# A decoder layer on one core: in the routed expert tiles, gate and up weights become the stationary operand, and the down product gets a second bank

## What is computed

```python
def _L0_ffn_ref(hidden_states, gate_w, sh_gate, sh_up, sh_down, rt_gate, rt_up, rt_down):
    x = hidden_states.reshape(-1, h)
    logits = x @ gate_w
    top_val = jnp.max(logits, axis=-1, keepdims=True)
    top_id = jnp.argmax(logits, axis=-1)
    score = jax.nn.sigmoid(top_val)
    xs = x * score
    g = jnp.einsum('th,ehi->eti', xs, rt_gate)      # H=128, I=256, E=8
    u = jnp.einsum('th,ehi->eti', xs, rt_up)
    act = jax.nn.silu(g) * u
    y = jnp.einsum('eti,eih->eth', act, rt_down)
    onehot = jax.nn.one_hot(top_id, E, dtype=x.dtype)
    routed = jnp.einsum('eth,te->th', y, onehot)
    shared = _swiglu(x, sh_gate, sh_up, sh_down)
    return (shared + routed).reshape(b, s, h)
```

## Time and profile before

| | |
|---|---|
| median of three runs | 648.67 us |
| the profiled execution, and the span of its trace | 643.3 us, 641.6 us |
| TensorE (PE) busy, share of the span | 593.4 us, 92% |
| VectorE (DVE) | 428.0 us, 67% |
| ScalarE (ACT) | 424.9 us, 66% |
| GpSimd (POOL) | 310.7 us, 48% |
| tail loop, first record transpose to last output scatter | 549.57 to 633.07 us |

### The profile page before, as it was taken

How to read it: one execution, slowest core, us unless ns; L and a number is a source line. 1 busy time by engine, 2 the same in 40 slices (tenths; PEclk the granted TensorE clock), 3 DMA queues, 4 the chain that set the end, 5 groups by cost and what they waited for, 6 DMA issues and landing times.

```text
span 641.6 us, 14968 instructions
## 1 busy us (share of the span) xinstructions
PE 593.4 (92%) x5231; PEld 514.1 (80%) x5231; DVE 428.0 (67%) x1185; ACT 424.9 (66%) x1512; POOL 310.7 (48%) x331
## 2 busy tenths in 40 slices
PE   3868999999999999999999999999999987999993
PEld 2767799889988998899989988998889876766661
DVE  3858665878685868586858685868564566376562
ACT  3538788777776787678677867786768764444551
POOL 3524644365336633663366336633652354147553
PEclk9969999999999999999999999999999998899997
DMA  7300000000010001000100000000000007325420
GB/s 161 98 18 13 17 2 2 13 18 2 2 30 18 17 3 30 18 18 2 30 18 17 1 15 17 17 2 2 17 18 1 2 27 227 115 72 157 144 74 8
DMA packets 24953, 23.49 MB, mean 37 GB/s; under 512 B 7007, under 2 KB 22497, under 8 KB 24880
## 3 DMA queue, kind: packets, MB, share of 16 engines
q1 hardware_dynamic: 20368, 14.91, 8.6%
q0 software_dynamic: 2784, 6.32, 2.7%
q10 hardware_dynamic: 1728, 1.32, 0.9%
HBM read 15.03 MB, written 7.95 MB: 36 GB/s over the span
## 4 chain that ended last, share of the span: by engine, by line
PE 70%; DVE 15%; ACT 7%; issue 3%; DMA 1%; POOL 1%; SPq 0%; DVEq 0%; POOLq 0%
PE bank L1128 9%; PE bank L1275 9%; PE bank L1243 8%; PE bank L1130 7%; PE bank L1129 7%; PE bank L1253 7%; PE bank L1264 5%; PE bank L1355 4%; ACT prob L1031 4%; PE bank L1224 2%; PE bank L1380 2%; PE bank L1135 2%; DVE stats L648 2%; DVE mneg L816 2%; ACT oT L1041 2%
## 5 line engine op out<-in xcount | busy, mean ns | idle before, releaser
L1031 ACT ACTIVATE prob<-bank,mneg 128x128 f32<-128x128 f32 x512 | 182.0, 376 | 80.1 <-DVE mneg L816 79.9
L560 POOL TENSOR_TENSOR prob<-prob,rden 128x512 f32<-128x512 f32 x128 | 130.7, 1041 | 107.1 <-DVE rden L823 106.8
L1031 ACT ACTIVATION_READ_ACCUMULATOR prob<-bank,mneg 128x1 f32 x512 | 109.8, 214 | 0.0
L1037 ACT COPY probT<-bank 128x512 f32<-128x512 f32 x128 | 76.8, 600 | 36.7 <-PE bank L1253 36.6
L816 DVE TENSOR_REDUCE mneg<-bank 128x4 f32<-128x512 f32 x128 | 80.3, 669 | 18.5 <-PE bank L1243 18.4
L1253 PE MATMUL bank<-ident,prob 128*128 128x128 f32 x512 | 78.4, 276 | 5.5 <-POOL prob L560 4.7
L499 POOL TENSOR_TENSOR rstd<-var_eps,neg_half 128x4 f32<-128x4 f32 x24 | 24.7, 1029 | 114.6 <-DVE var_eps L653 114.6
L1243 PE MATMUL bank<-kT,qT 64*128 64x128 f32 x1024 | 74.4, 285 | 2.9 <-issue 1.7
L1243 PEld LDWEIGHTS bank<-kT,qT 64*128 64x128 f32 x1024 | 62.2, 187 | 14.0 <-issue 11.4
L1253 PEld LDWEIGHTS bank<-ident,prob 128*128 128x128 f32 x512 | 60.6, 142 | 10.6 <-issue 6.2
L1264 PE MATMUL bank<-probT,V 128*64 128x128 f32 x1024 | 64.2, 279 | 0.0
(11 more groups left out here) (194 smaller groups left out, 1332.9 us busy)
## 6 DMA issues: line engine op xcount, KB each, us to landing
prob<-routed SPq DMA_DIRECT2D x39, 128.5 KB, 2.1
xin<-in_x_dram SPq DMA_DIRECT2D x8, 256.0 KB, 2.8
ctx_nat<-in_ctx_dram SPq DMA_DIRECT2D x8, 192.0 KB, 2.5
routed<-blank ACTq DMA_DIRECT2D x8, 128.5 KB
qT<-in_L_ffn_rt_gate_dram SPq DMA_DIRECT2D x1, 1024.0 KB, 5.9
qT<-in_L_ffn_rt_up_dram SPq DMA_DIRECT2D x1, 1024.0 KB, 11.1
out_dram<-probT,prob POOLq DMA_INDIRECT x39, 2.2
prob<-in_L_xattn_Wq_dram SPq DMA_DIRECT2D x1, 512.0 KB, 6.1
```

The costliest lines, as they stand in the source:

```text
L560: nc.gpsimd.tensor_tensor(view, view, spread(rden[:, m % 2, c * NC:(c + 1) * NC], 2, S), ALU.mult)\
L1031: last = nc.scalar.activation(prob[:, m % 2, p * S:(p + 1) * S], score_bank(m, c)[:, i * S:(i + 1) * S], ACT.Exp, bias=mneg[:, m % 2, p:p ...
L1037: nc.scalar.copy(probT[:, m % 2, c * 512:(c + 1) * 512], made(r1, ("T", m, c))[:])\
```

## The change

ScalarE copies each tile's gate and up weights, 128x512, from where the register points to one of three fixed places (`w4`: the two halves of `xin`, and `hw`, which nothing uses any more by then). With the address fixed, the weights can be the stationary operand, in four pieces of 128 columns, and the turned record moves. The product then comes out with the hidden units on the partitions, which is how the down product wants the activation: the two transposes L1371 and the copy L1110 are gone. The three gate and up banks go round (`gu_bank`), the down product alternates between two banks, and so D of a tile waits for `y_done` of the tile two before it. ScalarE copies one tile ahead: `copy_weights(0)` stands ahead of its loop, and `copy_weights(j + 1)` between R and H of step `j`; each reads `exp_tab` into a register first. TensorE still reads it too, for the down weights.

```diff
@@ -215,8 +215,10 @@
         rec = prob[:].rearrange("p a n -> p (a n)")[:, 0:RING * ROW].rearrange("p (a b) -> p a b", a=RING)
         recT = oT[:, 0, 0:2 * P].rearrange("p (a b) -> p a b", a=2)
         tanh4 = oT[:, 0, 2 * P:2 * P + 2 * I].rearrange("p (a b) -> p a b", a=2)
-        act4 = V[:, 0, 0:2 * I].rearrange("p (a b) -> p a b", a=2)
-        act4T = V[:, 0, 2 * I:4 * I].rearrange("p (a b) -> p a b", a=2)
+        act4 = V[:, 0, 0:3 * I].rearrange("p (a b) -> p a b", a=3)
+
+        w4 = [xin[:, 0].rearrange("p b n -> p (b n)"), xin[:, 1].rearrange("p b n -> p (b n)"),
+              hw[:].rearrange("p b n -> p (b n)")]
         yo = probT[:, 0, 0:RING * D].rearrange("p (a b) -> p a b", a=RING)
 
         EVEN = XH * S // ROW
@@ -409,8 +410,8 @@
         TABLE_1, TAILS, TABLE_2 = 15, 16, 27
 
 
-        gu_bank = [bank[2], r1.bank(("PV", B - 1, 0))]
-        at_bank = [r1.bank(("PV", B - 1, 1)), r1.bank(("out", B - 1))]
+        gu_bank = [bank[2], r1.bank(("PV", B - 1, 0)), r1.bank(("PV", B - 1, 1))]
+        down_bank = [bank[1], r1.bank(("out", B - 1))]
 
         block = ctx.enter_context(nc.Block())
 
@@ -955,14 +956,14 @@
 
             def activate(j):
                 dve.wait_ge(gu_tanh, j + 1)
-                ps = gu_bank[j % 2]
-                if j >= 2:
-
-                    dve.wait_ge(at_ready, j - 1)
-                nc.vector.scalar_tensor_tensor(out=act4[:, j % 2], in0=tanh4[:, j % 2], scalar=1.0, in1=ps[:, 0:I],
+                ps = gu_bank[j % 3]
+                if j >= 3:
+
+                    dve.wait_ge(dn_ready, j - 2)
+                nc.vector.scalar_tensor_tensor(out=act4[:, j % 3], in0=tanh4[:, j % 2], scalar=1.0, in1=ps[:, 0:I],
                                                op0=ALU.add, op1=ALU.mult).then_inc(act_half, 1)
                 dve.wait_ge(act_half, j + 1)
-                nc.vector.scalar_tensor_tensor(out=act4[:, j % 2], in0=act4[:, j % 2], scalar=0.5,
+                nc.vector.scalar_tensor_tensor(out=act4[:, j % 3], in0=act4[:, j % 3], scalar=0.5,
                                                in1=ps[:, I:2 * I], op0=ALU.mult, op1=ALU.mult)\
                     .then_inc(act_done, 1)
 
@@ -970,7 +971,7 @@
                 dve.wait_ge(dn_ready, j + 1)
                 if j >= RING:
                     dve.wait_ge(out_in[j % RING], 16 * (j // RING))
-                nc.vector.tensor_tensor(yo[:, j % RING, :], bank[1][:, 0:D], rec[:, j % RING, D:2 * D],
+                nc.vector.tensor_tensor(yo[:, j % RING, :], down_bank[j % 2][:, 0:D], rec[:, j % RING, D:2 * D],
                                         ALU.add).then_inc(y_done, 1)
 
             for j in range(TILES + 3):
@@ -1093,21 +1094,33 @@
                     for g, step in steps_at(ACT_F, F_AT, n, b):
                         ffn(g, step)
 
+            def copy_weights(j):
+                if j >= 3:
+
+                    act.wait_ge(gu_ready, j - 2)
+                if j == ROUND1:
+                    act.wait_ge(table, TABLE_2)
+                half, i = (0, j) if j < ROUND1 else (1, j - ROUND1)
+                e = act.value_load(exp_tab[0:1, half, i:i + 1], min_val=0, max_val=E - 1)
+                nc.scalar.copy(w4[j % 3], rt_gu[:, bass.ds(e * (2 * I), 2 * I)]).then_inc(w4_in, 1)
+
+            act.wait_ge(table, TABLE_1)
+
+            act.wait_ge(x1_in, NG)
+            act.wait_ge(wr_in, 16 * 3)
+            copy_weights(0)
             for j in range(TILES + 3):
                 if j < TILES:
                     act.wait_ge(ft_ready, j + 1)
                     nc.scalar.copy(recT[:, j % 2], bank[0][:, 0:P]).then_inc(ft_copied, 1)
+                if j + 1 < TILES:
+                    copy_weights(j + 1)
                 if 0 <= j - 1 < TILES:
                     act.wait_ge(gu_ready, j)
                     if j >= 3:
                         act.wait_ge(act_done, j - 2)
-                    nc.scalar.activation(tanh4[:, (j - 1) % 2], gu_bank[(j - 1) % 2][:, 0:I], ACT.Tanh,
+                    nc.scalar.activation(tanh4[:, (j - 1) % 2], gu_bank[(j - 1) % 3][:, 0:I], ACT.Tanh,
                                          scale=0.5).then_inc(gu_tanh, 1)
-                if 0 <= j - 2 < TILES:
-                    act.wait_ge(at_ready, j - 1)
-                    if j >= 4:
-                        act.wait_ge(dn_ready, j - 3)
-                    nc.scalar.copy(act4T[:, j % 2], at_bank[j % 2][:, 0:I]).then_inc(at_copied, 1)
                 if j < 2:
                     empty_PV(B - 1, j)
                 for step in ACT_TAIL.get(j, ()):
@@ -1345,15 +1358,22 @@
                         pe.wait_ge(ft_copied, j)
                     pe.transpose(bank[0][:, 0:P], rec[:, j % RING, 0:D], ident[:]).then_inc(ft_ready, 1)
                 if 0 <= j - 1 < TILES:
-                    e = held[j - 1]
                     if j == 1:
 
                         pe.wait_ge(exp_done, NC * B)
                     if j == 2:
                         vacate(("PV", B - 1, 0))
+                    if j == 3:
+                        vacate(("PV", B - 1, 1))
                     pe.wait_ge(ft_copied, j)
-                    pe.matmul(gu_bank[(j - 1) % 2][:], recT[:, (j - 1) % 2], rt_gu[:, bass.ds(e * (2 * I), 2 * I)],
-                              start=True, stop=True).then_inc(gu_ready, 1)
+                    pe.wait_ge(w4_in, j)
+                    if j > 3:
+
+                        pe.wait_ge(act_done, j - 3)
+                    for c in range(2 * I // P):
+                        last = pe.matmul(gu_bank[(j - 1) % 3][:, c * P:(c + 1) * P], w4[(j - 1) % 3][:, c * P:(c + 1) * P],
+                                         recT[:, (j - 1) % 2], start=True, stop=True)
+                    last.then_inc(gu_ready, 1)
                 if j < TILES:
 
                     if j == ROUND1:
@@ -1363,21 +1383,16 @@
                     prob_v(B - 1, j)
                 if j == 2:
                     out_product(B - 1)
-                if 0 <= j - 2 < TILES:
-                    if j - 2 < 2:
-                        vacate((("PV", B - 1, 1), ("out", B - 1))[j - 2])
-                    pe.wait_ge(act_done, j - 1)
-                    for h in range(I // P):
-                        last = pe.transpose(at_bank[j % 2][:, h * P:(h + 1) * P],
-                                            act4[:, j % 2, h * P:(h + 1) * P], ident[:])
-                    last.then_inc(at_ready, 1)
                 if 0 <= j - 3 < TILES:
                     e = held.pop(j - 3)
-                    pe.wait_ge(at_copied, j - 2)
-                    if j > 3:
-                        pe.wait_ge(y_done, j - 3)
+                    pe.wait_ge(act_done, j - 2)
+                    if j == 4:
+                        vacate(("out", B - 1))
+                    if j > 4:
+
+                        pe.wait_ge(y_done, j - 4)
                     for h in range(I // P):
-                        last = pe.matmul(bank[1][:, 0:D], act4T[:, (j - 3) % 2, h * P:(h + 1) * P],
+                        last = pe.matmul(down_bank[(j - 3) % 2][:, 0:D], act4[:, j % 3, h * P:(h + 1) * P],
                                          rt_dn[:, bass.ds(e * I + h * P, P)], start=(h == 0),
                                          stop=(h == I // P - 1))
                     last.then_inc(dn_ready, 1)
```

More of the change, by code:

```diff
@@ L284, in decoder_layer @@
         act_done = sem("activation_done")
-        at_ready = sem("activation_turned")
-        at_copied = sem("activation_turned_copied")
+        w4_in = sem("tile_weights_copied")
         dn_ready = sem("down_ready")
```

## The result

The change made the kernel slower where the result was taken: 654.26 us (median of 6 runs, 652.47 to 656.96) against 648.49 us for the kernel before (6 runs, 648.15 to 649.01), ratio 1.0093, 95% interval 1.0066 to 1.012. Forecast were 645.4 us and a range up to 650.6. The runs of the changed kernel spread over 4.5 us, those of before over 0.9 us.

A forecast was written before the change was run, and what follows sets the result against it. TensorE was taken to bound the kernel, setting the last stretch's step of 1.74 us. The terms 1.2 - 1.4 + 2.0 - 5.1 gave -3.3 us, so 648.67 - 3.3 = 645.4 us, eight-in-ten range 643.6 to 650.6.

The forecast's parts named there:

- the one on the base: Whole kernel: the runs' median lies 5.4 us above the profiled 643.3 us; -3.3 us was taken over unchanged from 648.67.
- TensorE's step: TensorE's work per routed tile in the tail: 1.46 us, 0.28 less, with six extra weight loads costed at nothing.
- the rival on loads: TensorE's weight loads are not hidden: 0.03 us per pass costs 9 us over 39 tiles, 654.8 us; chance 0.02.
- D's wait: Down product's wait for the tile before goes, 0.45 for 0.54 us; rival that it stays: -1.2, 647.5 us, chance 0.09.
- ScalarE's step: Per tile 1.43 us, from record copy through weights copy and H; with a region's end 2.27. Rival, ScalarE the bound: 0.17.
- First stretch: Tail steps 0 to 8, 22.61 us: the first weights copy makes ScalarE late and the lateness stays, +1.2 us.
- Second: Second stretch, tiles 9 to 13, 9.13 us: TensorE needs only the record copy of the tile before, -1.4 us.
- Third: Third stretch, tiles 13 to 18, 9.38 us: ScalarE sets the step, 5 x 2.27 = 11.35, +2.0 us.
- H to E: On ScalarE, from H to the DMA of a region's end, start to start: 0.69 to 0.79 us, taken as 0.74.
- Wait for tile 21: Last stretch: TensorE waits 0.8 us for tile 21's load, landing 5.96 us after the last region's end was issued.
- Fourth stretch: Last 21 steps, 36.47 us: 21 x 1.46 = 30.6, with a wait at tile 21 31.4, -5.1 us.
- The clock rival: In steps 12 to 16 TensorE's clock falls to half: -0.7 us in all, 648.0 us; chance 0.06.

The follow-up runs named there:

- 644 groups: Groups of runs, each on its own chip, where the kernel before took 643.9 to 644.6 us; the changed kernel gained 0.7% in the two that ran it.
- 648 group: The group of runs, on its own chip, where the kernel before took 648.3 us, as in the result; the changed kernel lost 1.1%.
- group 4: Runs on the chip where the kernel before took 648.29 us; the changed kernel, unedited, took 656.35 us, ratio 1.0106.
- group 2: Runs on a chip where the kernel before took 643.85 us; the changed kernel, unedited, took 639.59 us, ratio 0.9933.
- after_again: The changed kernel, unedited, run once more where the kernel before took 643.85 us: 639.59 us, ratio 0.9933.
- b_two_banks: The kernel before, with the down product alternating between two banks from routed tile 9 on, waiting for the tile before last: 641.41 us, ratio 0.9968.
- before_third: The kernel before, unedited, run for its profile on a chip where before took 644.34 us: 645.89 us (one run).
- changed_third: The changed kernel, unedited, run once more where the kernel before took 644.6 us: 640.12 us, ratio 0.9934.
- w_fixed_waits: The changed kernel with ScalarE always copying expert 0's weights, four satisfied waits per step replacing the register load and its three register instructions: 640.47 us, ratio 0.9941.
- w_reg_held: The changed kernel with ScalarE loading the expert's register once, at tile 0, and every copy of weights using that register: 638.15 us, ratio 0.9906.
- pe_fewer: The changed kernel with expert 0 for every tile, fixed addresses on ScalarE and TensorE, 28 TensorE instructions per step in place of 34: 638.03 us, ratio 0.9897.
- many_waits: The changed kernel with ScalarE always copying expert 0's weights, no register load, 16 satisfied waits per step (12 instructions, not 8): 639.62 us, ratio 0.9926.

## Why the prediction was wrong

**The step that failed is the one on the base**: "The median of the runs lies 5.4 us above that execution; I take the difference over unchanged." The trace shown, 643.3 us, is like those of the 644 groups; the times to be forecast were like the 648 group's. On the former the difference is -4.3 us (ratio 0.9933), 1 us more than forecast; on the latter it is +5.8 us in the result and +8.1 in group 4. Between the medians of the result and of group 2, the condition that the trace does not show costs the kernel before 648.49 - 643.85 = 4.6 us and the changed kernel 654.26 - 639.59 = 14.7. The prediction took these two for equal, and the 10 us between them turn -4.3 into +5.8. A gap of 5.4 us between the profiled execution and a median whose runs agree within 0.8 us was a row in the table, and I treated as a constant what depends on the kernel. It should have been a rival: what costs 5.4 us that this trace does not show, and will the change make it more?

**What the gap is.** Shown: in the profiles of the 648 kind ScalarE and VectorE go on up to 2.5 us late after TensorE's instructions about every fourth step, SyncE's queue is held up as well, and at 585 us TensorE stood for 4.5 us; this does not hang on ScalarE's instructions or on who issues the region ends. Comparing the two profiles of the changed kernel above, it costs 16.07 - 9.37 = 6.7 us in steps 13 to 17 and 33.36 - 24.72 = 8.6 us in the last 17. Some of the first is the clock. In the 6.8 us from 588.70, around the end of that long wait, the granted clock was 0.50, the level of 1.2 GHz:

```profile
588.70:595.50 6.80, 5.73 (x27) 5.76 (x28) 2.37 (x7) 3.22 (x8) 3.84 (x4) 0.50 0.36 118
```

Open: why the engines go on late, why on that chip, and whether the stall would be there without a profiler at work. That the recording causes it is a rival that nothing here excludes: the traces of these executions lack a seventh of the semaphore records that the others hold, all in the tail, and every execution here was recorded. A run of both kernels with no profiler on such a chip would decide it and was not made. That TensorE issues 34 instructions per 1.45 us in place of 26 per 1.73 fits, but was only argued. Nor is there a profile of the kernel before on such a chip, so that its own 4 us there were not seen.

**The terms, against after_again on a 644 chip and the earlier trace rows.**

- TensorE's step 1.46 us: 1.454. Right. The six more weight loads are hidden; the passes stand 0.11 us apart. So the rival on loads falls. The rule of the Trainium skill ("TensorE: Matmul & The Clock Gate", Part 3, The mechanism) that loads overlap running matmuls only where the row group differs does not hold for this kernel: its passes come at that distance with a load each.
- D's wait goes with a second bank: 0.09 forecast, 0.08 measured alone (b_two_banks). That rival falls.
- ScalarE's step: R to W 0.63 to 0.72 (0.65), W to H 0.53 (0.50), register load 0.28 (0.30). Right. The floor of about 600 ns for a `tensor_load` in the Trainium skill ("DMA: Bandwidth & Descriptors", Latency and other measured facts) does not hold for these loads: the 39 in the result's profile took 0.278 us in the middle and 0.469 at most.
- First stretch +1.2: +0.9 (23.51 - 22.61). That agrees but can't be told: in before_third, the kernel before again, this stretch took 24.79 us, T of tile 0 to T of tile 9. Second -1.4: -1.5 (7.58 against 9.13). Right.
- Third +2.0: 0.0 (9.37 against 9.38). Wrong term: H to E. It is 0.30 to 0.33 us, not 0.74, as ScalarE's queue runs the load for E beside W and H. The rows had C there, and the load started only as C did. Timeline of after_again:

```profile
583.15 0.38 ACT L1122 ACTIVATE oT<-bank 128x256 f32<-128x256 f32 x1
583.45 0.34 ACTq L1056 DMA_DIRECT2D routed<-blank  x1
583.83 0.27 ACT L1115 COPY oT<-bank 128x128 f32<-128x128 f32 x1 [0.30 <-issue]
584.55 0.62 ACT L1105 COPY xin<-qT 128x512 f32 x1 [0.46 <-issue]
585.08 0.38 ACT L1122 ACTIVATE oT<-bank 128x256 f32<-128x256 f32 x1
585.41 0.34 ACTq L1056 DMA_DIRECT2D routed<-blank  x1
585.79 0.27 ACT L1115 COPY oT<-bank 128x128 f32<-128x128 f32 x1 [0.34 <-issue]
```

- Wait for tile 21, 0.8 us: 6.57 - 3 x 1.454 = 2.2. The place was right, the releaser wrong: not the last region end, but GpSimd's last record scatter, "they keep up with 1.46" being untrue in the four steps that have two.
- Fourth stretch -5.1: its 17 steps from T of 21 to T of 38 give -4.76 (24.72 against 29.48), right; with the wait, T of 18 to T of 38 is 31.29 against 34.65, -3.4.
- Sum -3.3: -4.0 by T of tile 38 (71.75 against 75.77 from T of tile 0), -4.3 in the medians. That the sum comes so near is luck in part: the third stretch is 2.0 us better than its term and the fourth 1.7 worse, and they cancel. Two slips in the rivals, 0.1 us each, change nothing: five times 0.5 gives -0.8 and 647.9 us for the clock, and 5 us less give 643.7.
- The clock rival: 1.00 throughout in after_again, but 0.63 in the 4.5 us after changed_third's longer wait for tile 21, where the last 17 steps took 26.3 us in place of 24.7. w_fixed_waits, w_reg_held and pe_fewer show the same (0.63 to 0.65). This rival, put at steps 12 to 16, thus comes in at another place, and the wait is paid for twice:

```profile
588.67:595.86 7.19, 4.68 (x40) 4.48 (x39) 4.63 (x14) 4.10 (x11) 5.57 (x6) 1.00 0.33 105
595.86:600.40 4.54, 4.54 (x26) 4.54 (x27) 1.04 (x3) 2.15 (x6) 1.33 (x3) 0.63 0.54 145
```

## What to carry to other kernels

When the profiled execution and the median of the runs differ by more than the runs among themselves, the trace is of another condition than the times: forecast for both, and give the gap a rival of its own. A stall that recurs every so many instructions may only recur every so many steps; change that engine's instruction count alone before believing the first. And a change worth 0.7% on one chip and -1% on another wants runs on several chips: of the kernels here, b_two_banks, the second down bank alone, beats before by 0.3% and leaves TensorE's instruction count as it was, but it was run on one chip only, a 644 one.

## What the runs showed of the hardware that was not expected

- The same program, on chips of the same kind, differs in how soon an engine follows another: R starts 0.3 us after T on one, up to 2.8 us on the other (609.92 to 612.74 above), while the main loop takes as long on both (T of tile 0 at 550.42 and 549.71).
- The traces of the slower kind hold a seventh fewer semaphore records (4668 against 5429 for the same program), all missing from the tail.
- A satisfied wait on TensorE is not free: four such instructions of 0.05 us ahead of D made the step 0.33 us longer, while eight on ScalarE, which had room, in place of the register load and its three instructions, cost nothing (many_waits 0.9926, changed_third 0.9934).
- ScalarE's queue runs a register load beside the copy and the tanh ahead of it, so that H to E is 0.30 to 0.33 us here, where C to E in the earlier trace rows was 0.69.
